# A recurrence with a routed expert layer on one core: hidden products regrouped, a GpSimd-issued store, and the last triangular inverse split over two engines

## The reference, cut to what matters

```
xm = x + xx * (lo + time_maa)                 # four mixed inputs
r, k, v = xrg @ Wr.T, xk @ Wk.T, xv @ Wv.T
w2 = tanh(xwa @ decay_w1.T) @ decay_w2        # 64 hidden channels
kk = k + tanh(xk @ kkk_w1.T) @ kkk_w2         # then normed per head
a, ma, mk = sigmoid(...)                      # 16 hidden channels each
s = s * w + (s @ kk) * (-kk * a) + v * k      # per step and head
y = s @ r ; groupnorm ; + bonus ; * gate ; @ Wo.T
```

## Time and profile before

| | us |
|---|---|
| three timed runs | 1059.22, 1067.2, 1067.53 |
| median | 1067.2 |
| the profiled execution | 1076.19 |
| its span | 1074.1 |
| TensorE busy | 980.1 (91%) |
| VectorE busy | 768.0 (71%) |
| GpSimd busy | 613.1 (57%) |
| ScalarE busy | 519.9 (48%) |
| mean granted clock of TensorE | 0.951 |

### The profile page before, as it was taken

How to read it: one execution, slowest core, us unless ns; L and a number is a source line. 1 busy time by engine, 2 the same in 40 slices (tenths; PEclk the granted TensorE clock), 3 DMA queues, 4 the chain that set the end, 5 groups by cost and what they waited for, 6 DMA issues and landing times.

```text
span 1074.1 us, 42156 instructions
## 1 busy us (share of the span) xinstructions
PE 980.1 (91%) x16652; PEld 801.8 (75%) x16653; DVE 768.0 (71%) x1793; ACT 519.9 (48%) x1081; POOL 613.1 (57%) x1135
## 2 busy tenths in 40 slices
PE   8898989999999989999999998679899999999995
PEld 5676777777777767777777776557899898989894
DVE  5766788889879778887688885266476666666663
ACT  4474576677677576676476783221122121212120
POOL 1088786788886787785867876810133333333321
PEclk9997999999999999998799998689999999999998
DMA  5113225225324225224143133746545445544430
GB/s 121 40 21 81 71 33 110 65 51 111 77 47 101 70 44 111 72 42 107 17 101 87 28 91 85 206 115 232 217 163 176 161 174 162 176 158 170 158 119 4
DMA packets 208894, 112.14 MB, mean 104 GB/s; under 512 B 172508, under 2 KB 192224, under 8 KB 208352
## 3 DMA queue, kind: packets, MB, share of 16 engines
q1 hardware_dynamic: 202352, 100.92, 35.0%
q0 software_dynamic: 3744, 8.40, 2.3%
q10 hardware_dynamic: 2640, 0.54, 0.3%
HBM read 85.57 MB, written 26.08 MB: 104 GB/s over the span
## 4 chain that ended last, share of the span: by engine, by line
PE 61%; DVE 14%; issue 8%; POOL 6%; DMA 5%; ACT 4%; DVEq 1%; SPq 1%; ACTq 0%; POOLq 0%
PE bank L576 16%; PE bank L970 12%; PE bank L983 9%; PE bank L662 6%; PE ry L983 4%; PE bank L718 3%; POOL arena L1914 3%; POOL arena L1911 3%; DVE bank L1389 2%; PE ry L692 2%; PE bank L594 1%; PE bank L622 1%; PE bank L950 1%; PE ry L698 1%; PE bank L740 1%
## 5 line engine op out<-in xcount | busy, mean ns | idle before, releaser
L576 PE MATMUL bank<-arena 128*128 128x256 f32 (+2 forms) x992 | 280.9, 422 | 22.4 <-DVE arena L1434 9.5
L1914 POOL TENSOR_TENSOR arena<-arena 128x30 f32<-128x30 f32 (+14 forms) x480 | 261.6, 545 | 37.6
L1911 POOL TENSOR_TENSOR arena<-arena 128x30 f32<-128x30 f32 (+14 forms) x480 | 250.5, 522 | 36.4
L576 PEld LDWEIGHTS bank<-arena 128*128 128x128 f32 x992 | 178.5, 203 | 67.9 <-issue 31.5
L970 PEld LDWEIGHTS bank<-arena 128*128 128x128 f32 x1248 | 146.8, 194 | 5.8 <-issue 3.0
L970 PE MATMUL bank<-arena 128*128 128x128 f32 x1248 | 147.5, 277 | 3.1 <-DVE arena L1820 2.5
L1498 DVE TENSOR_TENSOR arena<-bank,arena 128x512 f32<-128x512 f32 x128 | 79.5, 684 | 53.1 <-PE bank L662 53.1
L1302 ACT ACTIVATE arena<-arena 128x1 f32<-128x1 f32 x39 | 11.5, 294 | 178.6 <-DVE arena L1774 178.6
L983 PE MATMUL bank<-arena 128*128 x416 | 96.4, 385 | 0.1
L1945 POOL COPY arena<-arena 128x1 int32 (+1 forms) x39 | 7.1, 183 | 146.4 <-DVE arena L1838 146.4
L983 PEld LDWEIGHTS bank<-arena 128*128 128x128 f32 x416 | 76.9, 190 | 14.5 <-issue 4.9
(11 more groups left out here) (173 smaller groups left out, 1757.7 us busy)
## 6 DMA issues: line engine op xcount, KB each, us to landing
arena<-in_W SPq DMA_DIRECT2D x47, 1024.0 KB, 5.1
...
```

The costliest lines, as they stand in the source:

```text
L576: mm = pe.matmul(ring.tile(m, name)[0:rows, to], lhsT, rhs, start=(i == 0), stop=(i == len(terms) - 1))
L1911: inv_ok.inc(f"m{s}", TT(t, U[:, 0:s, s:s + 1].broadcast_to(shape), U[:, s:s + 1, s + 1:TB].broadcast_to(shape), ALU.mult))
L1914: inv_ok.inc(f"a{s}", TT(U[:, 0:s, s + 1:TB], U[:, 0:s, s + 1:TB], t, ALU.add))
```

## The change

- **Two waves.** z is summed from two products over 32 rows each. `decay_a_kk` issues z (first half of its rows), a and kk, each from its own strip of 32 rows; `decay_ma_mk`, after the router, issues z (second half), ma and mk.
- **Keys.** The product kk is added in PSUM on top of k, which is made ahead of the gates. `sum_kk` is gone; ScalarE copies kk out (`keep_kk`) and squares it from the bank. ScalarE's order is a, logits, kk, square, z. VectorE's `decay_reads` comes after `bonus_terms`, ScalarE's `growths` before a copy of keys.
- **Banks.** The logits, the solved values and one copy of keys are in other banks. Three products with 512 columns become two with 256 each.
- **Store.** GpSimd starts the DMA that stores each inverse. SP only loads it (`heads_from_inverse`). The loads of block 14's inverse come straight after the read-back of block 15's scores.
- **Last inverse.** GpSimd inverts the left 24 columns, VectorE the right 8, in a PSUM bank, in three pieces within body `last`. ScalarE copies the left part of the system for both.
- **W2.** All eight loads come after the last inverse has landed.

```diff
+        CUT = 24
+        coefs = view(at_zt, CUT * CUT).rearrange("p (r c) -> p r c", r=CUT)
+        right = banks[2][:, 0:TB * (TB - CUT)].rearrange("p (r c) -> p r c", r=TB)
...
-        comb = Stage(sem("comb"), [(1, "kk scan t f k2 ls e2 kkn q ao bt k3 rk bm0 bm1 km0 km1 u wend")])
+        comb = Stage(sem("comb"), [(1, "scan t f k2 ls e2 kkn ao bt k3 rk q bm0 bm1 km0 km1 u wend")])
...
-        ring = Ring(banks, [(0, "bk00@5"), (1, "h@2"), (-2, "g@4"), (1, "k@3"), (0, "bk01@2"), (1, "z@1 a@5 kk@3 ma@4 mk@2"),
-                            (-3, "logit@3"), (-2, "wo@0"), (1, "ss@0"), (-1, "xa@1 xb@3"), (1, "r@4"),
-                            (0, "bk11@5"), (1, "v@2"), (0, "bk10@5 v0@1 v1@3"),
+        ring = Ring(banks, [(0, "bk00@5"), (1, "h@2"), (1, "k@3"), (-2, "g@4"), (0, "bk01@2"), (1, "a@5 kk@3"), (-3, "logit@0"),
+                            (1, "z@1 ma@4 mk@2"), (-2, "wo@0"), (1, "ss@0"), (-1, "xa@5 xb@3"), (1, "r@4"),
+                            (0, "bk11@1"), (1, "v@2"), (0, "bk10@5 v0@1 v1@3"),
                             (1, "rk@4"), (-1, "su@0"), (1, "sc00@2 sc01@5 sc02@3 sc03@1 tg@4"), (2, "lo1@5"),
                             (1, "sc10@2 sc11@5 sc12@1 sc13@4"), (-1, "yc@3"), (2, "lo2_1@2 lo2_2@5 lo2_0@0 lo2_3@1"),
...
-
-            def inverse_to_heads(m):
-
-                inv_ok.wait(sp, m, "a1")
-                if m:
-                    sp.wait_ge(u_in, m * 64)
-                sp.dma_start(ud, Up[m % 2].rearrange("p r c -> p (r c)")).then_inc(u_out, 16)
                 if m == last:
-                    load_tokens(last)
-                elif m and m - 1 < last - 1:
-                    load_tokens(m - 1)
+                    heads_from_inverse(last - 1)
+
+            def heads_from_inverse(m):
+
...
-                if has(n - 1):
-                    inverse_to_heads(n - 1)
+                if has(n - 1) and n != last:
+                    heads_from_inverse(n - 1)
                 if has(n - 3) and n <= last:
                     store_x1(n - 3)
-                if n == last:
+                if n == last + 1:
+                    sp.wait_ge(u_in, NBLK * 64)
                     load_experts(slice(0, 4))
-                if n == last + 1:
                     load_experts(slice(4, E))
...
             def decay_a_kk(m):
                 hid_act.wait(pe, m, "decay", "copy", "kkk")
-                from_hidden(m, [[("z", 2, slice(0, P), hid)]])
-                from_hidden(m, [[("a", 0, slice(64, 96), hid), ("kk", 0, slice(96, 128), kkh)]])
-
-            def ma_mk(m):
-                hid_act.wait(pe, m, "copy")
-                from_hidden(m, [[("ma", 1, slice(64, 96), hid), ("mk", 1, slice(96, 128), hid)]])
+                for name in ("z", "a", "kk"):
+                    ring.wait_empty(pe, m, name)
+                for h, to in both:
+                    mm_z = pe.matmul(ring.tile(m, "z")[:, to], w_out[0:32, 2, hs(h)], hid[0:32, :], start=(h == 0), stop=False,
+                                     skip_group_check=True)
+                    mm_a = pe.matmul(ring.tile(m, "a")[:, to], w_out[64:96, 0, hs(h)], hid[64:96, :], start=True, stop=True)
...
+            def decay_ma_mk(m):
+                pe.wait_ge(half_decay, m + 1)
+                for name in ("ma", "mk"):
+                    ring.wait_empty(pe, m, name)
+                for h, to in both:
+                    mm_z = pe.matmul(ring.tile(m, "z")[:, to], w_out[32:64, 2, hs(h)], hid[32:64, :], start=False, stop=True,
+                                     skip_group_check=True)
+                    mm_ma = pe.matmul(ring.tile(m, "ma")[:, to], w_out[64:96, 1, hs(h)], hid[64:96, :], start=True, stop=True)
+                    mm_mk = pe.matmul(ring.tile(m, "mk")[:, to], w_out[96:128, 1, hs(h)], hid[96:128, :], start=True, stop=True)
+                ring.fill(m, "z", mm_z)
...
+                if has(n + 1):
+                    square(n + 1, "k", 1, 2)
                 if has(n - 2):
                     gates(n - 2)
                 if n == last + 2:
                     keep_busy(2, idle_ps)
-                if has(n + 1):
-                    square(n + 1, "k", 1, 2)
                 if has(n) and n < last:
...
-                if has(n + 1):
-                    ma_mk(n + 1)
-                if -1 <= n <= 0:
-                    keep_busy(4, ry_bank[0])
                 if has(n - 3):
                     router(n - 3)
                 if n == last + 3:
                     keep_busy(2, idle_ps)
+                if has(n + 1):
+                    decay_ma_mk(n + 1)
+                if -1 <= n <= 0:
+                    keep_busy(4, ry_bank[0])
                 if has(n - 2):
...
+            def keep_kk(m):
+                if m:
+                    comb.wait(act, m - 1, "kkn")
+                ring.wait_full(act, m, "kk")
+                proj.inc(m, "kk", A(flat(kk), bank(m, "kk"), ACT.Copy))
 
...
+            def keep_coefs(m):
+                act.wait_ge(n_in, (m + 1) * 16)
+                last_inv.wait(act, 0, "diag")
+                comb.wait(act, m, "e2")
+                A(coefs, Up[m % 2][:, 0:CUT, 0:CUT], ACT.Copy).then_inc(coefs_kept, 1)
...
                 if has(n + 1):
+                    keep_a(n + 1)
+                if has(n - 3):
+                    keep_logits(n - 3)
+                if has(n + 1):
+                    keep_kk(n + 1)
+                    square_kk(n + 1)
                     keep_z(n + 1)
                     sigma_of_z(n + 1)
-                    keep_a(n + 1)
                     keep_ma(n + 1)
                     abs_of_z(n + 1)
-                if has(n - 3):
-                    keep_logits(n - 3)
                 if n == last + 1:
                     second_inverse_to_heads(last)
                 if has(n + 1):
-                    square_kk(n + 1)
...
-            def sum_kk(m):
-                ring.wait_full(dve, m, "kk")
-                proj.wait(dve, m, "k")
-                comb.inc(m, "kk", TT(flat(kk), ring.tile(m, "kk")[:, :], flat(kt), ALU.add))
...
+            def start_right(m):
+                dve.wait_ge(n_in, (m + 1) * 16)
+                last_inv.wait(dve, 0, "diag")
+                last_inv_dve.inc("start", nc.vector.tensor_copy(right, Up[m % 2][:, :, CUT:TB]))
+                dve.wait_ge(coefs_kept, 1)
+                proj.wait(dve, m, "iW0", "iW1")
+
+            def invert_right(m, steps):
+                U = Up[m % 2]
+                for s in steps:
+                    last_inv_dve.wait(dve, 0, "start" if s == TB - 2 else f"a{s + 1}")
+                    c = max(s + 1, CUT) - CUT
+                    n = TB - CUT - c
+                    shape = [P, s, n]
+                    t = flat(L)[:, 0:s * n].rearrange("p (r c) -> p r c", r=s)
+                    column = U[:, 0:s, s:s + 1] if s >= CUT else coefs[:, 0:s, s:s + 1]
+                    last_inv_dve.inc(f"m{s}", TT(t, right[:, s:s + 1, c:].broadcast_to(shape), column.broadcast_to(shape), ALU.mult))
+                    last_inv_dve.wait(dve, 0, f"m{s}")
+                    last_inv_dve.inc(f"a{s}", TT(right[:, 0:s, c:], right[:, 0:s, c:], t, ALU.add))
+
+            def keep_right(m):
+                last_inv_dve.wait(dve, 0, "a1")
+                last_inv_dve.inc("kept", nc.vector.tensor_copy(Up[m % 2][:, :, CUT:TB], right))
 
...
+                if n == last:
+                    start_right(last)
+                    invert_right(last, range(TB - 2, 23, -1))
                 if has(n - 1):
                     keep_x(n - 1, "a", 0)
                     keep_x(n - 1, "a", 1)
                     keep_x(n - 1, "b", 1)
+                if n == last:
+                    invert_right(last, range(23, 12, -1))
                 if has(n + 1):
                     normed_kk(n + 1)
-                    decay_reads(n + 1)
                     decay_kk(n + 1)
                     removal(n + 1)
                     decay_keys(n + 1)
                     bonus_terms(n + 1)
+                    decay_reads(n + 1)
                 if has(n + 1):
                     mask_removal(n + 1)
                     mask_keys(n + 1)
@@ -1690,6 +1740,9 @@
                     keep_scores(n + 1, 1, 3)
...
+                if n == last:
+                    invert_right(last, range(12, 0, -1))
+                    keep_right(last)
...
+            def invert_left(m):
+
+                pool.wait_ge(n_in, (m + 1) * 16)
+                U = Up[m % 2]
+                inv_ok.wait(pool, m - 1, "a1")
+                last_inv.inc("diag", nc.gpsimd.memset(U.rearrange("p r c -> p (r c)")[:, 0:TB * TB:TB + 1], 1.0))
+                pool.wait_ge(coefs_kept, 1)
+                for s in range(CUT - 2, 0, -1):
+                    n = CUT - 1 - s
+                    shape = [P, s, n]
+                    t = Ut[:, 0:s * n].rearrange("p (r c) -> p r c", r=s)
+                    if s < CUT - 2:
+                        last_inv.wait(pool, 0, f"a{s + 1}")
```

(20 more changed lines are left out.)

64 lines of the change are left out of this document (35 added, 29 removed).

## The result

| | before | changed |
|---|---|---|
| four runs each on one chip, us | 1059.22, 1067.2, 1067.53, 1077.75 | 1112.05, 1114.43, 1119.52, 1119.95 |
| median, us | 1067.4 | 1117.0 |
| ratio | | 1.047, 95% interval 1.039 to 1.055 |
| profiled execution, its span | 1076.2, 1074.1 | 1119.95, 1118.1 |

The change costs 50 us; I had forecast a gain of 9. Where it lies, counted from the start of a body (the first product of its hidden layer, as in the earlier trace rows): the fourth body starts 2.1 us later (131.9, now 134.0), the next eleven take 484.5 us instead of 452.6 (+31.9), the one after them 43.2 instead of 39.7 (+3.5), and from the start of the last to the last product it is 442.5 us instead of 437.3 (+5.2). Together that is 42.7 of the 44 us between the two profiled executions; the medians lie 50 us apart.

The account below looks back on a forecast made before the run. VectorE's work from scan to `keep_x` was taken to set the bodies, with TensorE waiting behind it. Terms -7.6 + 1.8 - 3.9 + 1 = -8.7 us took the median 1067.2 to 1058.5 us; own range 1053 to 1064, wider range 1043 to 1073.

Parts of the forecast that it names:

- the cost of nothing for TensorE on the path: Hidden products in each body: TensorE saves 1.2 to 1.7 us, counted as nothing because `keep_x` waits for VectorE.
- the term of -7.6 us for the twelve bodies: Twelve bodies with a router: eight gain 0.2 us each, four gain 1.5, mean 0.63, together -7.6 us.
- bodies A and B: Two profiled bodies before the change: router and projection take 2.86 us in A, 4.25 in B at 1.2 GHz.
- long stretches at 1.2 GHz in other places: Lower TensorE clock elsewhere, given 0.03 of the chance of a time slower than 1077.9 us.
- ScalarE's order and the scan: In each body the scan starts at 9.05 us instead of 7.75, and `keep_x` follows 6.05 us later at 15.1.
- Rival 2: ScalarE's longer path, z's copy behind the second wave, delays `keep_x` by 0.55 us in twelve bodies: 1076.4 us; chance 0.13.
- TensorE's waves: Hidden products: three strips run side by side, saving 0.86 us per body, and the wait ahead of the router goes.
- First three bodies: Bodies without a router: ScalarE's extra copy of 0.60 us lies ahead of z, +1.8 us.
- The last inverse: Tail: split between GpSimd and VectorE, its store starts 5.6 us earlier, less 1.7 for landing: -3.9 us.
- The store: GpSimd's store of each inverse: landing 4.5 us, +1.7 us on the last inverse, hidden in the bodies.
- W2: Tail: W2's transfer runs beside `solve` and read-out of block 15, costing 0 to +4.7 us, taken as +1.
- rival 3: W2's pause of 4.7 us moves into the tail, cancels its 3.9, bodies gain half: 1066 us; chance 0.20.

Follow-up runs that it names:

- e1_banks: The changed kernel with other bank numbers: the key norms in bank 1 instead of bank 0, banks 0 and 1 swapped behind them; ratio to the kernel before 1.017.
- e2_filler: The changed kernel with four extra 256-column products into idle bank 1 ahead of the norms from block 3 on; ratio to the kernel before 1.013.
- e6_before_wait: The kernel before, with the norms from block 3 on also waiting for the token statistics that follow `add_tokens` on VectorE; ratio 1.033.
- e10: The kernel before, with the bonus product from block 3 on also waiting for VectorE's key mask; ratio 1.012.
- e8: The changed kernel with norms in bank 1, z whole first, router between the hidden pairs, W2 after block 15's read-out; ratio to the kernel before 1.019.
- e9: As e8, with ScalarE's copy of keys moved back ahead of the key decay and growths; ratio to the kernel before 1.025.
- e14_z_late: The kernel before, with ScalarE's copy of z also waiting for the second pair of hidden products; ratio 1.036.
- e3_tail: The kernel before with only the change's tail parts: GpSimd's store, the split last inverse, W2 behind the last inverse's landing; ratio 1.002.

## Why the prediction was wrong

- *The step that failed* is the cost of nothing for TensorE on the path, with what it stands on: "The distance from `keep_x` to `scores` is nearly the same, 9.5 and 9.1 us, and VectorE works through it", and of TensorE "it comes early now, and I take 0.4 us off for that". It came late. I followed the later scan to `keep_x` and not to `add_tokens`, the operation that stands between them on VectorE, and did not ask who waits for it. TensorE does: norms and projection share bank 0. In the kernel before `add_tokens` itself waited for the projection, and this wait had one row, 0.86 us in one body. From `keep_x` to the scores it is now 11.2 us in the mean instead of 9.6, at a clock of 0.89 instead of 0.96, and the term of -7.6 us for the twelve bodies measured +35.4; without the wait (`e1_banks`) they measure +9.4. Shown by `e1_banks`, `e2_filler` and `e6_before_wait`.
- *The clock.* I read the lower clock as the cause of the difference between bodies A and B, and so as something to win back. I did not ask what a new pause would do; the nearest that I came is 0.03 for "long stretches at 1.2 GHz in other places". The Trainium skill, TensorE: Matmul & The Clock Gate (A second HAM failure mode), which I had weighed only in favour of the change, tells of brief idling that makes the clock swing; the trace agrees (18.3 us of new waits, clock from 0.96 to 0.89), and e10 adds that a longer pause elsewhere did not do it.
- *ScalarE's order and the scan.* The scan at 9.05 us was right (9.3 in the mean). So were the 6.05 us from there to `keep_x` and its 15.1 in the body shown (6.02 and 15.1); the means are 16.2 and 15.6 in the two profiles, since `keep_x` starts near 18 us in three of the eleven bodies of the first. Left out was a second bound: ScalarE's logarithm ends at 13.6 us, just as VectorE comes to the key exponent that needs it, so that VectorE has no idle time there in the changed kernel but has with z early (e8, e9). Rival 2 has the right place ("z's copy behind the second wave") and a price of 0.55 us per body, by way of `keep_x`. Without the norms' wait (`e1_banks`) `keep_x` is 0.1 us later and the body 0.8 longer, so its mechanism is not shown, and `e14_z_late` does not isolate it. Its total of 1076 is still 41 us short, since the norms' wait was in none of the cases.
- *TensorE's waves.* Three strips do run side by side, a wave takes 1.07 us (forecast 0.96) and the wait ahead of the router is gone, all as said. It bought nothing: what TensorE saved it spent waiting.
- *First three bodies*: +1.8 forecast, +2.1 measured.
- *The last inverse.* VectorE's three pieces lasted 4.2, 7.5 and 6.0 us (forecast 4.3, 7.8, 6.0), GpSimd's left part was done 7.6 us ahead of them, and the inverse was complete 5.1 us earlier (forecast 5.6).
- *The store.* Its last landing took 2.9 us, where I had 4.5; the estimate of 3.2 from the Trainium skill, DMA: Bandwidth & Descriptors (Anatomy of one DMA), was the nearer. The median of all sixteen is 4.7 us, most of them beside other transfers, so the size is not the whole of it; the bodies did not notice (`e3_tail`).
- *W2.* I took +1 of 0 to 4.7; it was a pause of 5.3 us on the path, rival 3's, in the result's profile, 2.5 in the other profile of the same kernel, and none in three variants that load W2 at the same place.

The last store, from the view of transfers over 735 to 739.5 us (issuing queue, count, KB each, us to landing):

```profile
scr_u<-arena POOLq DMA_DIRECT2D x1, 512.0 KB, 2.9
```

Sum against the sum: forecast -7.6 + 1.8 - 3.9 + 1; measured +35.4 in the twelve bodies, +2.1 in the first, +5.2 in the rest.
